# Gathering 125 rows a tile instead of 128 in a graph layer on one Trainium2 core

## What is computed

```python
h = gelu(edge_attr @ f_w0 + f_b0)      # [20000, 50] -> [20000, 128]
h = gelu(h @ f_w1 + f_b1); h = gelu(h @ f_w2 + f_b2); h = gelu(h @ f_w3 + f_b3)
W = h * cutoff(edge_length)[:, None]
xf = x @ lin1_w                        # [1250, 128]
msg = xf[src] * W                      # a row of xf for every edge
agg = segment_sum(msg, dst)            # [1250, 128]
out = gelu(agg @ lin2_w + lin2_b) @ lin_w + lin_b
result = layernorm(x + out)
```

## Time and profile before

| | us |
|---|---|
| median of 3 runs | 312.98 |
| lowest, highest | 311.64, 314.6 |
| the profiled execution, its whole time | 311.7 |
| its span in the profile | 309.9 |

### The profile page before, as it was taken

The page is one execution under the profiler, slowest core; times in us unless marked ns, Lnnn a source line. Parts: engine busy times, 40 slices in busy tenths (PEclk is TensorE's granted clock), DMA queues, the critical chain, the costliest instruction groups (busy, mean ns, idle before and its releaser), DMA issues.

```text
span 309.9 us, 3660 instructions
## 1 busy us (share of the span) xinstructions
PE 249.1 (80%) x990; PEld 161.5 (52%) x990; DVE 103.4 (33%) x218; ACT 113.4 (37%) x181; POOL 156.9 (51%) x168
## 2 busy tenths in 40 slices
PE   3697939966995997699399869939984994998990
PEld 3344625735663473566257456625743662665760
DVE  5612430514154051414324141432414052335015
ACT  2544412433353243335224433522442352355033
POOL 7671747374555737455473755546474645630000
PEclk9899985796598579659957965995696599569768
DMA  6530211122112212211221221121122202210002
GB/s 206 154 103 20 68 53 52 27 78 59 42 40 65 68 26 77 60 43 32 66 65 26 77 67 44 34 64 57 34 77 54 57 21 73 64 31 0 0 0 83
DMA packets 14483, 17.54 MB, mean 57 GB/s; under 512 B 6512, under 2 KB 11533, under 8 KB 14478
## 3 DMA queue, kind: packets, MB, share of 16 engines
q0 software_dynamic: 5120, 10.50, 12.9%
q1 hardware_dynamic: 8632, 6.39, 7.2%
q10 hardware_dynamic: 726, 0.59, 0.7%
HBM read 16.19 MB, written 1.28 MB: 56 GB/s over the span
## 4 chain that ended last, share of the span: by engine, by line
PE 67%; another core or an unknown queue 15%; issue 7%; DVE 6%; DMA 2%; DVEq 1%; ACT 1%; SPq 0%; ACTq 0%
PE ps_even L430 9%; PE ps_even L406 9%; PE ps_agg_even L443 8%; PE ps_even L421 8%; PE ps_odd L421 8%; PE ps_agg_odd L443 7%; PE ps_odd L430 7%; PE ps_even L416 3%; PE ps_odd L416 3%; DVE messages L606 2%; DMA tables<-in_edge_tables 2%; DVE pre L591 1%; PE ps_even L507 1%; PE ps_odd L497 1%
## 5 line engine op out<-in xcount | busy, mean ns | idle before, releaser
L272 POOL DMA_INDIRECT gathered<-xf_dram,src_idx x152 | 146.9, 967 | 113.8 <-DVE messages L606 65.6
L443 PE MATMUL ps_agg_even<-onehot,messages 125*128 125x64 f32 x160 | 29.4, 346 | 41.4 <-DVE messages L606 33.9
L319 ACT ACTIVATE h<-ps_even,biases_sb 128x500 f32<-128x500 f32 x61 | 41.1, 674 | 57.7 <-PE ps_even L421 36.4
L443 PEld LDWEIGHTS ps_agg_even<-onehot,messages 125*128 125x128 f32 x160 | 28.1, 259 | 52.8 <-issue 44.1
L319 ACT ACTIVATE h<-ps_odd,biases_sb 128x500 f32<-128x500 f32 x61 | 41.1, 674 | 37.0 <-PE ps_odd L421 26.6
L317 ACT ACTIVATE h<-pre 125x512 f32<-125x512 f32 x40 | 25.2, 630 | 74.3 <-DVE pre L591 56.5
L591 DVE TENSOR_TENSOR pre<-ps_even,row_b_sb 125x512 f32<-125x512 f32 x20 | 13.8, 692 | 86.7 <-issue 55.9
L430 PEld LDWEIGHTS ps_even<-w_mlp_sb,h 128*125 128x125 f32 x160 | 26.4, 249 | 21.3 <-issue 19.1
L443 PEld LDWEIGHTS ps_agg_odd<-onehot,messages 125*128 125x128 f32 x160 | 29.8, 263 | 13.1 <-issue 13.1
L406 PE MATMUL ps_odd<-edge_in,w_mlp_sb 50*128 50x500 f32 x42 | 31.8, 848 | 0.0
L406 PE MATMUL ps_even<-edge_in,w_mlp_sb 50*128 50x500 f32 x42 | 31.6, 841 | 0.2 <-issue 0.2
(11 more groups left out here) (99 smaller groups left out, 159.1 us busy)
## 6 DMA issues: line engine op xcount, KB each, us to landing
edge_in<-in_edge_attrT SPq DMA_DIRECT2D x42, 97.7 KB
gathered<-xf_dram,src_idx POOLq DMA_INDIRECT x152
xf_dram<-xf_sb SPq DMA_DIRECT2D x2, 256.0 KB
lin_xT_sb<-in_lin_xT SPq DMA_DIRECT2D x1, 369.0 KB
src_idx<-in_srcT SPq DMA_DIRECT2D x22, 4.0 KB
lin_xT_sb<-in_lin_xT SPq DMA_DIRECT2D x1, 320.0 KB, 3.5
w_mlp_sb<-in_w_mlp ACTq DMA_DIRECT2D x1, 256.0 KB
out<-normed SPq DMA_DIRECT2D x1, 256.0 KB
```

What stands on the lines that cost most here:

```text
L272: nc.gpsimd.indirect_dma_start(out=gathered[:, b, t, :], out_offset=None, in_=xf_dram[:, :], in_offset=bass.IndirectOffsetOnAxis(ap=src_id ...
L319: nc.scalar.activation(out_ap, in_ap, GELU, bias=biases_sb[:, layer:layer + 1]).then_inc(done, 1)
L443: last = nc.tensor.matmul(ps_agg[b][:, 0:WINDOW], messages[:, slot, t, :], onehot[:, p % 2, b * TILES_PER_GROUP + t, :], start=(t == 0), s ...
```

## The change

Each gather of L272 names the first 125 partitions, of its destination and of its indices. The padded rows are no longer fetched. The eight gathers of the first pair (L264), the tables, the semaphores and their counts stay as they are.

```diff
                     nc.gpsimd.indirect_dma_start(
-                        out=gathered[:, b, t, :], out_offset=None, in_=xf_dram[:, :],
-                        in_offset=bass.IndirectOffsetOnAxis(ap=src_idx[:, b // 2, col:col + 1], axis=0),
+                        out=gathered[0:TILE, b, t, :], out_offset=None, in_=xf_dram[:, :],
+                        in_offset=bass.IndirectOffsetOnAxis(ap=src_idx[0:TILE, b // 2, col:col + 1], axis=0),
                     ).then_inc(gather_landed[b], 16)
```

## The result

| | before | after |
|---|---|---|
| median of four runs | 312.31 us (311.58 to 314.6) | 272.73 us (268.62 to 275.22) |
| ratio, 95% interval | 1 | 0.8643 [0.8522, 0.8764] |
| profiled execution, its span | 311.7 us, 309.9 us | 275.22 us, 273.3 us |

A time is the median of a kernel's executions, while a ratio and its interval leave out executions more than 1.5% above the fastest of their kernel, so a ratio can differ from the quotient of two medians.

A forecast was written before the change was run, and what follows sets the result against it. It took TensorE to bound low-clock stretches and a hold until gathers land to bound high-clock pairs. Holds ahead of the loop, 1.1 us, plus slip in it, 1.1, made 311.7 into 313.9; put on the median, 315.0, range 307 to 332.

The forecast's parts named there:

- What bounds the kernel: Main loop: TensorE bounds low-clock stretches; high-clock pairs end when their gathers land, 13.6 us a pair.
- Step (a): GpSimd's descriptor work per gather: taken as 0, with ends of -0.02 and +0.40 us.
- step (c): Gather's spread over DMA engines: five equal shares of 25 rows, landing 0.53 us later, ends 0 and +3.65.
- rival C: Gathers on GpSimd: dearer descriptors make it the bound; 335 us at +0.15 us a gather, 372 at +0.40; chance 0.15.
- Step (b): Bytes on the gather queue: 0.23 MB fewer, from 10.50 to 10.25 MB, worth nothing by itself.
- Step (d): Hold on TensorE's signals: later landings cost 1.1 us ahead of the loop and 1.1 us once in it.
- rival D: Hold on TensorE's signals: fewer engines per gather lift it or release it earlier; 301 us, down to 274; chance 0.13.
- The clock: Loop's alternating clock, 27.3 us per low and high stretch: assumed to keep its pattern and absorb later landings.
- "slower" of 0.39: Whole kernel: chance of a time above 316.1 us, beside same 0.48 and faster 0.13.
- B: Holds in and ahead of the loop: later landings add up, 5.3 us, 318.3; one engine 331 to 349; chance 0.12.

The follow-up runs named there:

- session 2: Second session, kernel before and changed kernel both run again unchanged: 312.14 us median before, 273.26 us changed, ratio 0.8853.
- pace kernel: Kernel before with all 128 rows plus a small GpSimd fill after each gather: 248.4 us beside 239.14, 314.43 us beside 312.14.
- session 3: Third session, changed kernel run again unchanged beside the kernel before at 238.43 us: 267.37 us, ratio 1.1474.

## Why the prediction was wrong, by its steps

**What bounds the kernel.** The reading of before was right for its setting: four of the idle microseconds in a high-clock pair came from a hold on TensorE's signals. I took it as a fixed property of the kernel. It is not: the same program took 238 us in three of the five sessions, and the kernels profiled beside it have no hold. Nor does a gather in flight hold the signals by itself: in the kernel after gathers follow each other without a pause, and the bias steps are on time.

**Step (a), descriptor work on GpSimd.** This term was mis-sized. I took 0 with ends of -0.02 and +0.40 us; it measured +0.25, in every run of the change. Rows of the trace before could not give the number, as no other row count stood there. The prediction named the cause of the spread in step (c), five engines instead of sixteen, and did not ask whether GpSimd, which issues the gather, pays for that as well. The table says it does, by the rows of one share and not by all the rows: 100 rows cost more than 128. By rival C's own count this decides who bounds the kernel, at 0.08 us and beyond, and after shows just that: GpSimd runs without a pause, and the messages wait for it. C's count of the time does not hold, though: for +0.25 us it would give a pair of 13.6 + 8 x 0.25 = 15.6 us, because it kept the 1.46 us ahead of the first gather and the landing in the pair. In the kernel after both are passed over, and the pair takes eight steps of 1.50 us.

**Step (b), bytes.** Worth nothing, as said. The queue fell from 10.50 to 10.43 MB, and not to 10.25, because of the small packets told of at the table: there are 7,296 packets more than before. A gather of 128 rows has only sixteen packets of 4 B besides its sixteen of 4,096 B.

**Step (c), the spread.** Right: five engines, 25 rows each, and the landing half a microsecond later (2.31 and 2.42 us from GpSimd's end to the index load; 2.3 to 2.4 was the forecast). The Trainium skill's rule (DMA: Bandwidth & Descriptors, section "Why a DMA increments its semaphore by 16 and not by 1") is borne out by the packets for these gathers, and its exception for direct copies does not show up in them. In the 238 us setting, from issue to landing, the median is 2.5 us with 112 rows, 3.3 with 125 and 7.8 with 127. Less what GpSimd takes longer (0.27 and 1.62 us), that is 0.5 and 3.7 us more, where 0.53 and 3.65 were counted for five engines and for one.

**Step (d), who pays.** This is the step that failed. I said that the hold would last until the later landing, and that the clock would absorb it, for 2.2 us more. The hold went away instead, but for two bias steps under 1 us: from 46.3 us in sum to 3.2, and from 40.5 to 2.6 in session 2. Who pays for the gathers is then GpSimd's own pace. The vanished hold is the mechanism of rival D, which had 0.13 and lay outside the range. Its number of 274 us came close (272.73), and that is luck in part: D counted a pair at 11.5 us with cheap gathers, and the real pair takes 12.0 with dear ones. The result is D's lifting down to C's bound: nineteen pairs of 12.0 us are 228 of the 273, and the rest lies ahead of the loop and behind it.

**The clock.** The prediction said that a changed pattern would break it. It changed: 6.83 us of low clock for each 17.07 of high, instead of equal parts.

**The sign.** The prediction's "slower" of 0.39 rested on B and C. In the 238 us setting C's mechanism is what happens, at 1.1474 [1.136, 1.1587]. In the 312 us setting the lifting of the hold outweighs it, 0.8643 and 0.8853.

**What stays open.** Why the hold is there in one setting and not in the other, and which part of the change lifts it: the use of five engines at a time, or the step of 1.50 us. The pace kernel was to part them and reached only 1.28 us; 100 and 119 rows met only the other setting. One trait of the traces goes with the setting. The trace of a kernel holds 4,480 to 4,524 records of semaphore updates in the 238 us setting (4,804 with the pace), and 1,964 to 2,228 in the 312 us setting for all kernels but the change, which has 2,532 and 2,522. So over half of these records are missing wherever the hold is, and 44% where it is lifted. Missing records would also explain that the kernel after has "issue" where the same kernel in session 3 has TensorE as the releaser. A jam on the way by which these records leave the core, which holds back TensorE's signals as well, would fit. That is an argument and no proof: no run took the records away. The Trainium skill (NOTIFIC — the notification-queue block, section "Overflow: three behaviours, one of which stalls the engine") has one kind of overflow that stalls the engine; no run here shows that it happened.

## What to carry to other kernels

When an indirect gather fetches a partial tile, divide the row count by its largest divisor up to sixteen and keep the quotient small: 128 or 112 rows cost GpSimd some 0.93 to 0.95 us here, 125 rows 1.20 and 127 rows 2.54, so dropping three padding rows can cost more than they do. When the chain has a large share with an unnamed releaser, repeat the unchanged kernel at another time before pricing anything on it, because here it took 238 or 312 us by the session and the sign of the change hung on that. An unnamed or missing releaser can be checked against the times themselves: how long after its producer's end does the step start? A change that wins by lifting such a hold is to be shown in both settings before it is kept.

## What the runs showed of the hardware

GpSimd's time for one indirect gather of 512 B rows follows the rows in one share, which is the row count by its largest divisor up to sixteen: 925 ns at 7 rows, 947 at 8, 982 at 9, 996 at 10, 1,089 at 17, 1,196 to 1,199 at 25 and 2,542 at 127. With fewer than sixteen shares, small packets of 32 B appear beside the data, 33 in a gather of 125 rows and 225 in one of 127. And one program on one chip took 239 us in one session and 312 in the next, with a granted clock of 0.93 to 0.97 in the one setting and 0.77 to 0.80 in the other, while a kernel that GpSimd bounds (the change) differed by only 2% between them.
